# Attention with the running sum weighted on GpSimd, a cleared region and a sum moved

## The reference

```
x = x + 0.5 * ffn(layernorm(x))
x = x + attn(layernorm(x))
x = x + 0.5 * ffn(layernorm(x))

attn:  delta, Bs, Cs, residual = split(x @ W_proj.T, 4)
       delta = softplus(delta @ W_delta.T + b_delta)
       y  = exp(delta * A1) * B1 * sum(x * Cs)          # sums over the sequence
          + cumsum(delta * B1) * sum(Cs)
       return y + residual * D

ffn:   top-1 router over 32 experts, capacity C = 640 rows each
       rows sorted into slots, y = (silu(xs @ w_gate) * (xs @ w_up)) @ w_down
       out = x + gate * y for accepted rows, x for the others
```

## Time and profile before

| | us |
|---|---|
| median of 3 runs | 1561.3 (1559.84 to 1561.47) |
| the profiled run's own time | 1561.85 |
| its span | 1560.0 |
| PE busy | 1301.6 (83%) |
| DVE busy | 1250.8 (80%) |
| ACT busy | 1098.8 (70%) |
| POOL busy | 678.0 (43%) |

### The profile page before, as it was taken

One profiled execution on the slowest core, in us unless ns is written; L12 is line 12 of the kernel. 1 busy time (PEld: TensorE's weight loads), 2 busy tenths in 40 slices (PEclk: granted clock), 3 DMA queues, 4 the chain that ended last, 5 costly groups with the idle time before them and its releaser, 6 DMA issues. The chain is left out here.

```text
span 1560.0 us, 31181 instructions
## 1 busy us (share of the span) xinstructions
PE 1301.6 (83%) x10179; PEld 1232.9 (79%) x10179; DVE 1250.8 (80%) x3385; ACT 1098.8 (70%) x2343; POOL 678.0 (43%) x778
## 2 busy tenths in 40 slices
PE   5545209999999999599999999987539999999996
PEld 4323108999999999599888889887439999999996
DVE  8959807999999999288999999999837777777775
ACT  6756307777777776489888889886647777777773
POOL 0566762443444334312245644544633444334443
PEclk9776558999999999799999999998859999999999
DMA  9995346666677662731111222111244444444440
GB/s 326 402 378 184 138 149 223 223 231 211 210 228 226 222 211 79 241 110 42 41 47 49 87 91 80 60 59 53 65 140 133 119 131 136 137 141 124 146 126 24
DMA packets 149775, 234.72 MB, mean 150 GB/s; under 512 B 24333, under 2 KB 124390, under 8 KB 147568
## 3 DMA queue, kind: packets, MB, share of 16 engines
q1 hardware_dynamic: 121968, 188.24, 37.2%
q0 software_dynamic: 27648, 44.50, 8.3%
HBM read 128.51 MB, written 136.48 MB: 170 GB/s over the span
## 5 line engine op out<-in xcount | busy, mean ns | idle before, releaser
L1027 PE MATMUL ps<-xs,ws 128*128 128x320 f32 x3072 | 465.1, 311 | 2.0 <-issue 2.0
L1027 PEld LDWEIGHTS ps<-xs,ws 128*128 128x128 f32 x3072 | 455.4, 189 | 2.8 <-issue 2.8
L1027 PE MATMUL ps<-ws,hs 128*128 128x256 f32 x1920 | 261.8, 288 | 10.8 <-DVE x L958 7.1
L851 POOL DMA_INDIRECT slots_and_rows<-x x160 | 164.6, 1028 | 243.2 <-DVE x L968 203.5
L851 POOL DMA_INDIRECT out<-x x160 | 157.8, 987 | 247.8 <-DVE x L958 166.7
L1027 PEld LDWEIGHTS ps<-ws,hs 128*128 128x128 f32 x1920 | 238.9, 190 | 24.0 <-issue 22.3
L890 ACT ACTIVATE x<-x 128x256 f32<-128x256 f32 x320 | 165.0, 594 | 58.2 <-DMA x<-slots_and_rows 43.7
L979 DVE TENSOR_TENSOR hf<-ps,sg 128x320 f32<-128x320 f32 x256 | 125.2, 489 | 88.3 <-ACT sg L911 87.7
L872 ACT CAST xs<-ps 128x512 fp32r<-128x512 f32 (+1 forms) x192 | 98.3, 513 | 131.0 <-PE ps L1020 131.0
L373 POOL DMA_INDIRECT slots_and_rows<-x,slot x128 | 126.9, 991 | 98.3 <-issue 86.5
L373 POOL DMA_INDIRECT slots<-x,slot x128 | 132.4, 1035 | 79.7 <-issue 44.3
(11 more groups left out here) (137 smaller groups left out, 2318.1 us busy)
## 6 DMA issues: line engine op xcount, KB each, us to landing
slots<-blank SPq DMA_DIRECT2D x16, 1310.0 KB
slots_and_rows<-blank SPq DMA_DIRECT2D x32, 655.0 KB, 4.5
x<-slots_and_rows SPq DMA_DIRECT2D x31, 655.0 KB, 3.9
x<-slots SPq DMA_DIRECT2D x31, 655.0 KB, 4.3
x<-slots_and_rows SPq DMA_DIRECT2D x32, 516.0 KB, 8.7
x<-in_x SPq DMA_DIRECT2D x32, 512.0 KB, 9.4
wraw<-in_w_gate SPq DMA_DIRECT2D x64, 256.0 KB, 2.7
wraw<-in_w_up SPq DMA_DIRECT2D x64, 256.0 KB
```

Of the source, the lines that this page charges most:

```text
L851: nc.gpsimd.indirect_dma_start(out=rows, out_offset=bass.IndirectOffsetOnAxis(ap=factor(e, k, F_ID).bitcast(U32), axis=0), in_=XG[:, e % G ...
L1027: ins = pe.matmul(dst, left(a, k), right(b, k), start=(n == 0), stop=(n == len(terms) - 1))
```

## The change

Three edits. In `route`, six of the sixteen blank stores stay ahead of SP's last eight loads and ten go behind them. In `experts`, `y_sum(e, 0)` goes ahead of `x_lo(e + 1, 1)` on VectorE. In `attention`, GpSimd multiplies the running sum by v into a new tile CS (`weight`), first in each step; the exponential's bias is A times b_delta alone; `mix` is the exponential times u plus CS; and PE turns the mixed tile with the identity, ahead of the residual's products, as turns that open the accumulation. `size_bias`, DIAG and the steps that made sign and size go.

```diff
+                FILL_FIRST = 6
...
-                    for n in range(NFILL):
+                    for n in range(FILL_FIRST):
                         fill2(sp, n)
                     for q in range(4 * XR, NQ4):
                         if q % 4 == 0:
                             sp.wait_ge(tail.scattered[q // 4 - XR], 16 * TB)
                         stream.load(sp, q)
+                    for n in range(FILL_FIRST, NFILL):
+                        fill2(sp, n)
...
                         if more:
+                            y_sum(e, 0)
                             x_lo(e + 1, 1)
-                        if more:
-                            y_sum(e, 0)
                             y_sum(e, 1)
...
+                    def weight(n):
+                        pool.wait_ge(scanned.sem, scanned.at(n + 1))
+                        if n % NC == 0:
+                            pool.wait_ge(factors.sem, factors.at(n // NC + 1))
+                        if n >= 2:
+                            pool.wait_ge(mixed.sem, mixed.at(n - 1))
+                        apart(pool)
+                        for h in range(HC):
+                            ins = nc.gpsimd.tensor_scalar(CS[:, n % 2, h, :], CC[:, n % 2, h, :],
+                                                          UV[:, n // NC % 2, 1, h:h + 1], None, ALU.mult)
+                        ins.then_inc(weighted.sem, 1)
+
                     for S in range(FIRST, LAST + NC):
+                        for n in at(S, PLUS):
+                            weight(n)
...
-                    def size_bias(a):
-                        act.wait_ge(sized.sem, sized.at(a + 1))
-                        act.activation(LB[:, a % 2, 0, :], UV[:, a % 2, 4, :], ACT.Ln).then_inc(size_links.sem, 1)
...
                             ins = act.activation(YT[:, n % 2, h, :], AB[:, n % 2, h, :], ACT.Exp,
-                                                 bias=LB[:, a % 2, 1, h:h + 1], scale=A1[:, h:h + 1])
+                                                 bias=ABD[:, h:h + 1], scale=A1[:, h:h + 1])
...
-                        dve.scalar_tensor_tensor(uv[:, 2, :], uv[:, 0, :], -1.0, uv[:, 0, :], ALU.mult, ALU.max)
-                        dve.tensor_scalar(uv[:, 5, :], uv[:, 0, :], 0.0, 2.0, ALU.is_ge, ALU.mult).then_inc(f_links.sem, 1)
...
-                        for h in range(HC):
-                            ins = dve.tensor_scalar(DIAG[:, a % 2, h, :], IDENT, uv[:, 6, h:h + 1], None, ALU.mult)
-                        ins.then_inc(diag.sem, 1)
-                        dve.wait_ge(f_links.sem, f_links.next())
+                        dve.sem_inc(factors.sem, 1)
...
                     def mix(n):
-                        dve.wait_ge(scanned.sem, scanned.at(n + 1))
+                        dve.wait_ge(weighted.sem, weighted.at(n + 1))
                         dve.wait_ge(da_done.sem, da_done.at(n + 1))
                         apart(dve)
                         for h in range(HC):
-                            ins = dve.scalar_tensor_tensor(YT[:, n % 2, h, :], CC[:, n % 2, h, :],
-                                                           UV[:, n // NC % 2, 3, h:h + 1], YT[:, n % 2, h, :],
+                            ins = dve.scalar_tensor_tensor(YT[:, n % 2, h, :], YT[:, n % 2, h, :],
+                                                           UV[:, n // NC % 2, 0, h:h + 1], CS[:, n % 2, h, :],
                                                            ALU.mult, ALU.add)
...
                         for j in range(CH):
+                            for h in range(HC):
+                                pe.matmul(ps[:, BY, j * H + h * P:j * H + (h + 1) * P],
+                                          YT[:, n % 2, h, j * P:(j + 1) * P], IDENT, start=(j + h == 0), stop=False,
+                                          is_transpose=True, skip_group_check=True)
+                        for j in range(CH):
                             for i, (a, b, k) in enumerate(terms):
-                                pe.matmul(..., start=(i == 0), stop=False, skip_group_check=True)
-                            for h in range(HC):
-                                ins = pe.matmul(..., YT[:, n % 2, h, j * P:(j + 1) * P], DIAG[:, t % 2, h, :],
-                                                start=False, stop=(h == HC - 1), skip_group_check=True)
+                                ins = pe.matmul(..., start=False, stop=(i == len(terms) - 1), skip_group_check=True)
```

More of the change, by code:

```diff
@@ L1081, in attention @@
                 SPARE = BLANK[:].rearrange("p k d -> p (k d)")
-                DIAG = SPARE[:, 0:2 * HC * P].rearrange("p (a c d) -> p a c d", a=2, c=HC)
-                PRODS = SPARE[:, 2 * HC * P:4 * HC * P]
-                LB = s([P, 2, 2, HC])
+                PRODS = SPARE[:, 0:2 * HC * P]
+                CS = s([P, 2, HC, CT])
                 NG = H + 1 + P + 1
@@ L1111, in attention @@
                 da_done = count("b_da", 2)
-                diag = count("a_diagonals")
-                sized = count("a_size")
-                biased = count("a_bias")
+                factors = count("a_factors")
+                weighted = count("b_weighted")
                 mixed = count("b_mixed")
                 residual_done = count("b_residual", 3)
-                size_links = Links(sem("a_size_log"))
                 x_added = count("b_x", 1)
@@ L1255, in softplus @@
                         act.activation(AB[:, n % 2], AB[:, n % 2], ACT.Ln, bias=1.0).then_inc(log_done.sem, 1)
-                    def size_bias(a):
-                        act.wait_ge(sized.sem, sized.at(a + 1))
-                        apart(act)
-                        act.activation(LB[:, a % 2, 0, :], UV[:, a % 2, 4, :], ACT.Ln).then_inc(size_links.sem, 1)
-                        act.wait_ge(size_links.sem, size_links.next())
-                        for h in range(HC):
-                            ins = act.activation(LB[:, a % 2, 1, h:h + 1], LB[:, a % 2, 0, h:h + 1], ACT.Identity,
-                                                 bias=ABD[:, h:h + 1])
-                        ins.then_inc(biased.sem, 1)
                     def d_a(n):
-                        a = n // NC
-                        if n % NC == 0:
-                            act.wait_ge(biased.sem, biased.at(a + 1))
                         act.wait_ge(softplus_done.sem, softplus_done.at(n + 1))
@@ L1281, in scalar @@
                                 tail.act_rstd(act, n // 2)
-                        for a in batches(S, 2):
-                            size_bias(a)
                         for n in at(S, PLUS):
@@ L1379, in scan @@
                         if n >= 2:
-                            dve.wait_ge(mixed.sem, mixed.at(n - 1))
+                            dve.wait_ge(weighted.sem, weighted.at(n - 1))
                         for h in range(HC):
@@ L1496, in residual @@
                     def residual(n):
-                        t = n // NC
-                        if n % NC == 0:
-                            pe.wait_ge(diag.sem, diag.at(t + 1))
                         pe.wait_ge(mixed.sem, mixed.at(n + 1))
@@ L1502, in residual @@
                         for j in range(CH):
-                            for i, (a, b, k) in enumerate(terms):
[L1504 to L1508, removed]
-                                                start=False, stop=(h == HC - 1), skip_group_check=True)
+                            for h in range(HC):
[3 more added lines that the diff above has]
+                        for j in range(CH):
+                            for i, (a, b, k) in enumerate(terms):
+                                ins = pe.matmul(ps[:, BY, j * H:(j + 1) * H], XS[:, n % 3, a, k, j * P:(j + 1) * P],
+                                                WA[:, 4 + 2 * b + k, :], start=False, stop=(i == len(terms) - 1),
+                                                skip_group_check=True)
                         ins.then_inc(residual_done.sem, 1)
```

## The result

The changed kernel takes 1664.3 us (median of 6 runs, 1662.71 to 1664.9) against 1561.4 us: 1.0658 times the time before, 95% interval 1.0644 to 1.0672. The forecast was 1583.8 us, the range 1562 to 1618. The sign was right, the size was wrong by a factor of 4.6 (22.5 us forecast, 102.9 measured).

The account below looks back on a forecast made before the run. The prediction took PE to bound the experts, GpSimd's scatters the end of routing, and VectorE attention. -13.1 - 22.3 - 8.0 + 71.7 - 9.8 + 4.0 = +22.5 us gave 1583.8 us, range 1562 to 1618.

Parts of the forecast that it names:

- Clearing, -13.1 us: Routing: with ten stores behind the last loads, GpSimd wins its idle time, -13.1 us (between 0 and -18.3).
- Sum, -22.3 us: Experts: the earlier sum removes PE's 0.36 us idle before the third pair, 62 times, -22.3 us (0 to -24.8).
- Attention, +57.9 us: Attention's terms: -8.0 off VectorE, +71.7 hand-over, -9.8 covered ScalarE waits, +4.0 GpSimd's queue; PE's saving not counted.
- part 3 (c): Attention: `weight` at 0.45 us an operation (bounds 0.22 to 0.86), hand-over 1.30 us against 0.18, 64 times, +71.7 us.
- (d): Attention, GpSimd's queue: `weight` behind roots and scatters makes a step 1.0 us late in four batches, +4.0 us.
- a_factors: Attention: a chain of 1.0 us taken from VectorE once in each of 8 batches, -8.0 us.
- PE's saving counted as nothing: Attention: four turns replace four DIAG products, at most 0.6 us a step, counted as nothing because PE waits for VectorE.
- short hand-over: Rival in attention: GpSimd at the fill's rate, hand-over 0.84 us, in all -7.0 us, 1555 us; chance 0.14.
- PE as the bound: Rival in attention: PE is the bound, the stall is hidden and PE's saving counts, 1526 down to 1488 us; chance 0.04.
- GpSimd slow under load: Rival in attention: operations of 0.86 us, hand-over 2.12 us, in all +75.0, 1637 us; chance 0.10.
- The clock: Rival in attention: TensorE's lower clock hits one step in eight, 4.2 us each, +33.6, 1618 us; chance 0.10.
- a mark of 0.9: Sign in attention: a granted clock under 0.9 between 700 and 1000 us would bring in the clock rival.

Follow-up runs that it names:

- e10: Kernel before with the clearing edit alone, on a chip like the first: 1547.8 us, 0.9916 times the time before.
- e1: Kernel before with the clearing edit alone, on a chip where the kernel before took 1635.9 us: 1636.5 us, 0.9997 times the time before.
- e12: Kernel before with clearing and sum edits, first turn's last-tile moments after the next expert's third pass instead of the first: 1531.5 us, 0.9815 times the time before.
- e4: Changed kernel, but `mix` reads the unweighted running sum and waits for the scan only; GpSimd's weighted copy goes unread: 1598.5 us, 0.9775 times the time before.
- e6: Changed kernel with `weight` doing 128 of the 256 columns of each half: 0.605 us an operation, attention 633.7 us; whole time not read.
- e5: Changed kernel with `weight`'s factor a constant in the instruction instead of a value per partition: 0.850 us an operation, attention 668.1 us; whole time not read.
- e7: Changed kernel with `mix` further down VectorE's step, behind the previous pair's new x and statistics: 1691.8 us, 1.0141 times the time before on its chip.
- e8: Changed kernel with `mix` last in VectorE's step, behind the router steps too: 1688.0 us, 1.0101 times the time before on its chip.
- e3: Changed kernel with the clearing and sum edits undone, so the attention edit alone: 1763.8 us, 1.0758 times the time before on its chip.

## Why the prediction was wrong, point by point

**Clearing, -13.1 us.** Right: -13.3 by the last scatter, -13.1 by e10. The argument that VectorE wins 18.3 us and GpSimd only its own pause held to 0.2 us. It holds on a chip on which the loads are what is late; e1 shows another on which the edit is worth nothing.

**Sum, -22.3 us.** Right in the second turn (11.5 us against 11.2), too much in the first (6.6). The failed half-sentence is "it catches up within the expert". In the first turn VectorE has the row moments. The changed kernel's waits between 240 and 600 us:

```profile
ACT hs L882 <- DVE hf L982: 18.4, 30, 0.6
...
PEld ps L1029 <- issue: 5.5, 30, 0.2
```

VectorE is up to 0.6 us late with the product of gate and up, and 0.18 us of the 0.36 come back on PE as a wait inside the gate and up products. e12 moved one operation and the wait only changed its place, which speaks for VectorE's load as its cause.

**Attention, +57.9 us, measured +134.4.** The mechanism was right: e4 removes VectorE's wait and leaves GpSimd's products and PE's turns, and 129.1 us come back. The step that failed is the price of the operation in part 3 (c): "I take 0.45, nearest to 0.19 + 0.22". It is 0.92. I took the slope from a fill, 0.87 ns a column; the changed kernel and e6 show 2.48 ns a column for a multiplication that also reads, with 0.29 us fixed, and e5 shows 0.07 us of it for the factor in memory. The hand-over is 2.27 us in place of 1.30: 64 x 0.97 = 62 us of the 76.5 that were missing (134.4 less 57.9). Even the upper bound of 0.86 was none: it put the worst fixed time together with the fill's slope, and the slope was what was wrong. The 0.38 us given beside it as an estimate was lower still.

GpSimd's queue, (d), was priced at 4.0 us and is 156.4 - 64 x 2.27 = 11.1 us. It is nearly all in five steps: `mix` waits 4.83 us at 834.69, 4.84 at 909.98, 4.83 at 985.12, 5.29 at 1060.74 and 4.10 at 1223.95, and 2.22 to 2.27 us everywhere else. The first four are the fullest steps that (d) had in mind. In the second of them both roots and two scatters stand ahead of `weight`:

```profile
903.75 1.39 DVE L1371 TENSOR_TENSOR_SCAN a<-vec,a 128x256 f32<-128x256 f32 x2
...
905.52 1.11 POOL L373 DMA_INDIRECT slots<-x,slot  x1 [0.38 <-issue]
...
906.94 0.98 POOL L373 DMA_INDIRECT slots<-x,slot  x1 [0.30 <-issue]
...
907.95 1.85 POOL L1200 TENSOR_SCALAR a<-a 128x256 f32<-128x256 f32 x2
...
909.98 0.88 DVE L1380 SCALAR_TENSOR_TENSOR a<-a 128x256 f32<-128x256 f32 x2 [4.84 <-POOL a L1200]
```

The scan ends at 905.14, and `weight` starts 2.81 us later in place of 0.24. So (d) had the right steps and priced them at 1.0 us each; they cost 2.6 to 3.0.

With the covered waits for ScalarE and the scan (17.5 us before, none after) and a_factors the account is 156.4 - 17.5 - 8.0 = 130.9 of 134.4 us. The 8.0 is the forecast's, and the traces bear it out: from the first `mix` to the last VectorE's time without its waits is 425.9 us before (447.9 less 22.0) and 417.9 after (577.1 less 159.2). The 3.5 us that are left lie behind the last `mix`: from there to the first scatter of the second experts it is 57.8 us before and 63.4 after, for a reason that stays open. With it the 76.5 us are complete: 62.1 of the hand-over, 7.1 of the queue, 3.5 behind the last `mix`, and 3.8 because the forecast took off 0.18 us in all 64 steps where the trace before has 7.7 us in 44.

**PE's saving counted as nothing.** Right: e4's attention is 4.4 us shorter than with DIAG (e1), less than the 8.0 of a_factors.

**The rivals.** The short hand-over failed because the fill's rate did not hold. PE as the bound failed because VectorE waits in all 64 steps and PE waits for it. "GpSimd slow under load" had the nearest time (1637) but not the cause: the operation is slow with VectorE standing still. It had a chance of 0.10, and the true time lay beyond it. The clock did fall. The changed kernel at the places where I had set a mark of 0.9:

```profile
700.00:800.00 100.00, 76.09 (x617) 69.93 (x618) 71.61 (x177) 71.39 (x147) 40.11 (x63) 0.96 0.09 33
...
900.00:1000.00 100.00, 79.19 (x566) 74.00 (x566) 68.92 (x173) 63.16 (x130) 61.01 (x82) 0.85 0.22 65
```

Steps at the lower level exist: the residual's twelve products (L1494) take 2.42 us at 855.49 (granted clock 0.69 from 855 to 858 us) and 1.68 us at 863.43 (1.00 from 863 to 866). But PE waited 115.0 us for `mix` in the stage, and VectorE, which sets the pace, did not wait for PE once between 647 and 1225 us: a slower PE had nothing to hold up there, and the account closes to 3.5 us without the clock. The Trainium skill's sentence (TensorE: Matmul & The Clock Gate, PE-mode transpose) that turns don't count as work for the gate does not explain the fall here: in e4 the same turns run among the same products at a granted clock of 0.95 to 1.00.

The Trainium skill (GPSIMD Engine Reference, Engine selection) advises against GpSimd for elementwise work, with the exception that an operation with one input is roughly at line rate. The advice held. The exception did not: GpSimd's operation with one input takes 0.922 us, against 0.482 us on VectorE for half of `mix`, which has two inputs of the same 256 columns.

## What to carry to other kernels

When two neighbours in the order of the engine that bounds a stage are split by a detour over another engine, the price is the whole detour, each time: here 0.24 + 1.85 + 0.18 us, 64 times. A price for an operation that the trace doesn't show has to come from one that moves data the same way, read and write; a fill bounds it from below only, and it was the slope, not the fixed part, that had to be bounded from above. Moving the waiting operation further down its engine's list, as e7 and e8 did, gives back only a part: another engine may then wait for it. Edits that come together are worth measuring apart: two of these three gain 2%, and the third hid it.

## What the runs showed of the hardware that was not expected

A TENSOR_SCALAR on GpSimd over 128 partitions in f32: 0.605 us for 128 columns, 0.922 us for 256, 0.850 us for 256 with a constant factor. In e4, where VectorE works meanwhile, the operation on 256 columns takes 1.027 us on average between 700 and 1100 us and VectorE's scan 0.757 us; in e3, on the same chip, where VectorE stands still while GpSimd multiplies, they take 0.925 and 0.731 us.

The same program took 1561, 1636 and 1670 us on three chips. The second turn of experts is the same on all (380.0 to 380.1 us with the old order, on two of them, and 368.5 to 368.8 with the new); from the first chip to the second, routing and the first turn make up much of the difference (last scatter at 227.5 or 243.2, first turn with the old order 378.0 or 418.6 to 419.1), and attention another 17 us (538.1, 554.9). Why the chips differ stays open.
